# An adaLN block with linear attention and MoE: tail norms, routing and scatters between the last encoder steps, expert outputs scattered to token order

## The reference

```python
h = layernorm(x) * (1 + ca) + sa
x = x + ga * encoder(h)            # 4 layers
h = layernorm(x) * (1 + cb) + sb
x = x + gb * ffn(h)

# encoder layer: causal linear attention, 16 heads of 8, chunks of 128
q, k, v = h @ Wq + bq, h @ Wk + bk, h @ Wv + bv     # feature map elu + 1 on q and k
h = ln(h + attention(q, k, v) @ Wo + bo) * g1 + be1
h = ln(h + gelu(h @ W1 + b1) @ W2 + b2) * g2 + be2  # 512 hidden
# after the last layer: ln(h) * gf + bef

# ffn: 16 experts, two per token, 640 places per expert, plus a shared MLP
probs = softmax(h @ router_w + router_b)
vals, idx = top_k(probs, 2); vals = vals / (sum(vals) + 1e-9)
pos = (cumsum(one_hot(idx)) * one_hot(idx)).sum(1) - 1   # place in the expert, in token order
expert_in[idx, pos] += h * (pos < 640)
expert_out = (silu(expert_in @ wg) * (expert_in @ wu)) @ wd   # 176 hidden, per expert
out = h + shared_mlp(h) + sum over two of expert_out[idx, pos] * vals * (pos < 640)
```

## Time and profile before

| what | us |
| --- | --- |
| times of three runs | 1343.13, 1343.81 (median), 1349.38 |
| the profiled execution | 1346.05 |
| its span, first to last instruction | 1344.3 |
| PE busy in the span | 1049.5 (78%) |
| DVE busy | 970.3 (72%) |
| POOL busy | 895.0 (67%) |
| ACT busy | 580.2 (43%) |
| mean granted TensorE clock | 0.887 |

### The profile page before, as it was taken

One profiled execution on the slowest core, in us unless ns is written; L12 is line 12 of the kernel. 1 busy time (PEld: TensorE's weight loads), 2 busy tenths in 40 slices (PEclk: granted clock), 3 DMA queues, 4 the chain that ended last, 5 costly groups with the idle time before them and its releaser, 6 DMA issues.

```text
span 1344.3 us, 22639 instructions
## 1 busy us (share of the span) xinstructions
PE 1049.5 (78%) x4916; PEld 691.2 (51%) x4916; DVE 970.3 (72%) x2224; ACT 580.2 (43%) x1441; POOL 895.0 (67%) x1258
## 2 busy tenths in 40 slices
PE   2769899999998999899999999985326959999000
PEld 1445566656665666566656665654224536666000
DVE  3889789999999999999999999984654423332122
ACT  2335555555555555555555555544521112221000
POOL 4768877787778777887778777865827771000675
PEclk9889999999999999999999999998556969898555
DMA  8411010001000100010001000000002223331222
GB/s 237 164 63 72 24 39 23 23 31 39 23 23 31 39 23 23 31 39 23 28 26 39 23 31 23 31 16 17 16 4 73 81 66 111 110 106 55 66 70 60
DMA packets 53358, 68.20 MB, mean 51 GB/s; under 512 B 12184, under 2 KB 30024, under 8 KB 53200
## 3 DMA queue, kind: packets, MB, share of 16 engines
q1 hardware_dynamic: 44702, 54.21, 12.1%
q0 software_dynamic: 4096, 8.40, 2.2%
q10 hardware_dynamic: 4530, 5.26, 1.1%
HBM read 24.03 MB, written 16.80 MB: 30 GB/s over the span
## 4 chain that ended last, share of the span: by engine, by line
PE 37%; issue 19%; POOL 18%; DVE 16%; ACT 4%; DMA 3%; DVEq 1%; POOLq 1%; ACTq 0%; SPq 0%
PE ps L1141 10%; PE ps L1192 5%; POOL expert_in_scratch L693 4%; PE ps L1182 3%; POOL w L726 3%; DVE prod L1414 3%; PE ps L789 3%; PE ps L788 2%; DVE red L1427 2%; PE ps L1130 2%; POOL rstd L1068 2%; PE ps L739 2%; DVE kvm L1430 2%; PE ps L737 2%; POOL xg L1096 1%
## 5 line engine op out<-in xcount | busy, mean ns | idle before, releaser
L1141 PE MATMUL ps<-kv,tri 128*128 128x384 f32 x768 | 289.7, 516 | 2.3 <-DVE prod L1414 2.3
L1051 POOL TENSOR_TENSOR kv<-qk,v 128x1152 f32<-128x1152 f32 x128 | 280.4, 2191 | 2.9 <-DVE qk L1408 2.9
L1141 PEld LDWEIGHTS ps<-kv,tri 128*128 128x128 f32 x768 | 144.7, 202 | 101.1 <-issue 36.8
L1414 DVE TENSOR_TENSOR prod<-ps,qk 128x1152 f32<-128x1152 f32 x128 | 172.4, 1347 | 25.4 <-PE ps L1141 24.7
L1427 DVE TENSOR_REDUCE red<-prod 128x144 f32<-128x1152 f32 x128 | 172.0, 1344 | 3.3
L1192 PE MATMUL ps<-x1T,w1s 128*128 128x512 f32 x256 | 135.7, 612 | 8.0 <-ACT hT L1303 4.8
L1182 PE MATMUL ps<-w,hT 128*128 (+1 forms) x1024 | 137.9, 285 | 0.0
L1182 PEld LDWEIGHTS ps<-w,hT 128*128 128x128 f32 x1024 | 127.0, 195 | 1.5
L1437 DVE TENSOR_TENSOR att<-tot,rden 128x128 f32<-128x128 f32 x128 | 110.1, 860 | 7.0 <-DVE rden L1434 0.2
L1130 PE MATMUL ps<-wqkv,xT 128*128 (+1 forms) x256 | 111.3, 518 | 0.0
L1275 ACT ACTIVATE ex<-ps 128x256 f32<-128x256 f32 x128 | 48.6, 380 | 133.2 <-PE ps L1130 133.2
(11 more groups left out here) (215 smaller groups left out, 2295.4 us busy)
## 6 DMA issues: line engine op xcount, KB each, us to landing
x1s<-X SPq DMA_DIRECT2D x32, 256.0 KB, 2.3
w1s<-w SPq DMA_DIRECT2D x32, 256.0 KB, 2.3
xs<-X SPq DMA_DIRECT2D x31, 256.0 KB, 2.3
expert_in_scratch<-room SPq DMA_DIRECT2D x16, 320.0 KB, 3.4
kv<-expert_in_scratch SPq DMA_DIRECT2D x16, 320.0 KB, 2.9
expert_out_scratch<-kv ACTq DMA_DIRECT2D x16, 320.0 KB, 2.6
mod<-mod_scratch SPq DMA_DIRECT2D x1, 2304.0 KB, 8.9
x<-in_L_attn_x_dram SPq DMA_DIRECT2D x8, 256.0 KB, 5.9
```

Source lines behind the costliest of these rows:

```text
L1051: pool.tensor_tensor(kv[:, n, :].rearrange("p (e h d) -> p e h d", e=EV, h=H), qk[:, n, 1, :].rearrange("p (h d) -> p h d", h=H).unsqueeze ...
L1141: mm = pe.matmul(ps_cum[:, j, :], tri[:, :], kv[:, n, j * CB:(j + 1) * CB], start=True, stop=True)
L1414: dve.tensor_tensor(prod[:, :].rearrange("p (b e c) -> p b e c", b=3, e=3), ps_cum.rearrange("p b (e c) -> p b e c", e=3), qk[:, n, 0, :]. ...
```

## The change

Tail step j now stands behind body 28 + j (`FIRST_TAIL`), so tail steps 0 to 6 alternate with bodies 28 to 34, of which 28 to 31 are full bodies, and 7 to 10 follow. Routing goes in four groups of 8 tiles, behind tail steps 4, 6, 8 and 10; the counts of earlier groups are carried in `sel_before`. The scatter of row b stands behind tail step 5 + b (rows 6 and 7 behind the last), with its loads on SP and its indirect DMAs on POOL. The shared FFN and the experts still follow.

The scattered rows are 130 wide: h, the place in token order that the output has to go to (home), and the weight. `finish` multiplies by the weight that lies in `xes`; `home_rows` on DVE makes the list of destinations; POOL scatters each expert's output by 5 indirect DMAs to `expert_out_scratch`, now in token order and zeroed at the start by 16 DMAs of 256 KB. SP reloads a place of `xes` only when the transposes, the home rows and the finish of the expert that was in it are done. At the end each row takes two plain loads instead of 8 gathers, and three DVE operations of 512; ACT stores the result. `add_h` moves from POOL to DVE, inside experts 1 to 8. Second down-projections now use all 128 rows, padded with zeros, in place of 48. Some tiles get memory of their own (`hT_all`, `f_xn`, `g_xn`), and loops behind the encoder are unrolled.

```diff
+        FIRST_TAIL = STEPS - B + 4
+        GROUPS = ((0, 2), (2, 4), (4, 6), (6, 8))
...
-            with engine.Fori(4 * NT, (STEPS - 1) * NT, NT) as i:
+            with engine.Fori(4 * NT, FIRST_TAIL * NT, NT) as i:
                 body(i)
-            for k in range(STEPS - 1, STEPS + 3):
-                body(k * NT)
-                for j in DRAIN[k - STEPS + 1]:
-                    tail_step(j)
-            for j in range(DRAIN[-1][-1] + 1, B + 3):
-                tail_step(j)
-                if j == ROUTE_AFTER:
-                    route(0)
-            route(1)
+            for k in range(FIRST_TAIL, FIRST_TAIL + B + 3):
+                if k < STEPS + 3:
+                    body(k * NT)
+                j = k - FIRST_TAIL
+                tail_step(j)
+                for g in routed_after(j):
+                    route(g)
+                if j >= 5:
+                    scatter(j - 5)
+            for b in range(B - 2, B):
+                scatter(b)
...
+        def sp_rows(sp, b):
+            par = b % 2
+            if b == 0:
+                sp.wait_ge(p_done, TILES * L)
+            sp.wait_ge(q["h_ready"], b + 1)
+            wait(sp, scat[par], b // 2 * 128)
+            for k in range(2):
+                sp.dma_start(hs2[:, par, :, k, 0:D], Hr[:, b * NT:(b + 1) * NT, :]).then_inc(hs2_load[par], 16)
...
             def expert_rows(e, par):
                 wait(sp, q["xet_ps"], e - 1)
-                sp.dma_start(xes[:, par, :], xe_tiles[ds(e, 1)].rearrange("a p c -> (a p) c")).then_inc(xe_load[par], 16)
+                wait(sp, q["yidx_ready"], e - 1)
+                wait(sp, q["ye_sb"], e - 1)
+                sp.dma_start(xes[:, par, :, :].rearrange("p j c -> p (j c)"), xe_tiles[e]).then_inc(xe_load[par], 16)
...
             for par in range(2):
-                sp.wait_ge(scat[par], B * 64)
-            sp.wait_ge(q["ua_ps"], B)
+                sp.wait_ge(scat[par], B // 2 * 128)
+            sp.wait_ge(q["xsh_done"], TILES)
...
+            for b in range(B):
+                wait(sp, q["mix1_done"], b - 1)
+                for k in range(2):
+                    sp.dma_start(yg[:, b % 2, k, :, :], ye_tokens[b, :, k, :, :]).then_inc(yg_load[b % 2], 16)
...
+        def pool_scatter(pool, b):
+            par = b % 2
+            if b == 0:
+                pool.wait_ge(q["xe_zeroed"], 16 * E)
+            pool.wait_ge(q["route_ready"], b // 2 + 1)
+            wait(pool, scat[par], b // 2 * 128)
...
+            for n in range(NT):
+                for k in range(2):
+                    pool.indirect_dma_start(
+                        out=xe_dram, out_offset=bass.IndirectOffsetOnAxis(ap=scat_u[:, b * NT + n, k:k + 1], axis=0),
+                        in_=hs2[:, par, n, k, :], in_offset=None).then_inc(scat[par], 16)
...
+            for e in range(E):
+                par = e % 2
+                pool.wait_ge(q["yidx_ready"], e + 1)
+                pool.wait_ge(q["ye_sb"], e + 1)
+                for j in range(CT):
+                    pool.indirect_dma_start(
+                        out=ye_dram, out_offset=bass.IndirectOffsetOnAxis(ap=yidx[:, par, j:j + 1], axis=0),
+                        in_=yes[:, par, j, :], in_offset=None).then_inc(ysc[par], 16)
...
-                    mm = pe.matmul(o, ehid_b[0:FB, par, j * P:(j + 1) * P], ewd[0:FB, par, 1, :], start=False, stop=True)
+                    mm = pe.matmul(o, ehid_b[:, par, j * P:(j + 1) * P], ewd[:, par, 1, :], start=False, stop=True)
...
             def finish(e, par):
                 dve.wait_ge(q["ye_ps"], e + 1)
-                wait(dve, ye_store[par], ((e - par) // 2) * 16)
-                dve.tensor_copy(yes[:, par, 0:4 * P], down_bank[:, 0, :])
-                dve.tensor_copy(yes[:, par, 4 * P:CAP], down_bank[:, 1, 0:CAP - 4 * P]).then_inc(q["ye_sb"], 1)
+                wait(dve, ysc[par], e // 2 * CT * 16)
+                for j in range(CT):
+                    ins = dve.tensor_scalar(yes[:, par, j, :], down_bank[:, j // 4, (j % 4) * P:(j % 4 + 1) * P],
+                                            xes[:, par, j, D + 1:D + 2], None, ALU.mult)
+                ins.then_inc(q["ye_sb"], 1)
```

More of the change, by code:

```diff
@@ L252, in head_row, with steps @@
             return None
-        def steps(engine, body, head_step, tail_step, route):
+        def steps(engine, body, head_step, tail_step, route, scatter):
             head_step(0)
@@ L347, in adaln_block_kernel @@
         down_bank = ps[:, 6:8, :]
[L349 to L374, removed]
-        def sp_tail(sp):
[L378 to L386, removed]
+        def sp_rows(sp, b):
[6 more added lines that the diff above has]
+                sp.dma_start(hs2[:, par, :, k, 0:D], Hr[:, b * NT:(b + 1) * NT, :]).then_inc(hs2_load[par], 16)
+        def sp_tail(sp):
             def expert_weights(e, par):
-                wait(sp, q["ua_ps"], B + 2 * e - 2 if not isinstance(e, int) or e > 1 else 0)
-                gate, up = (w[ds(e, 1)].rearrange("a k f -> (a k) f") for w in (w_gate, w_up))
+                wait(sp, q["ua_ps"], B + 2 * e - 2 if e > 1 else 0)
+                gate, up = w_gate[e], w_up[e]
                 sp.dma_start(ewg[:, par, 0:F], gate).then_inc(ew_load[par], 16)
@@ new lines, in dve_route @@
+            dve.scalar_tensor_tensor(out=room_a, in0=before, scalar=float(CAP - 1), in1=over_tiles(expert_base),
+                                     op0=ALU.min, op1=ALU.add).then_inc(q["cnt_read"], 1)
+            dve.wait_ge(q["cnt_read"], g + 1)
+            if g < len(GROUPS) - 1:
+                then(dve.tensor_reduce(sel_row[:, :], selb[:, part, :].rearrange("p t e -> p e t"), AXX, ALU.add))
+                if g == 0:
+                    dve.tensor_copy(sel_before[:, :], sel_row[:, :])
+                else:
+                    dve.tensor_tensor(sel_before[:, :], sel_before[:, :], sel_row[:, :], ALU.add)
@@ L796, in expert @@
                 hidden(e, par, 0)
-                if not isinstance(e, int) or e > 0:
+                if e > 0:
                     down(e - 1, 1 - par)
-                if not isinstance(e, int) or e < E - 1:
+                if e < E - 1:
                     transposes(e + 1, 1 - par)
                 hidden(e, par, 1)
-            experts(pe, expert)
+            for e in range(E):
+                expert(e, e % 2)
             down(E - 1, 1)
@@ L812, in shared_gates @@
                 act.activation(sil_b[0:FB, :], ps[0:FB, 1, :], ACT.Silu).then_inc(q["esb_done"], 1)
-            rows(act, shared_gates, 1, B)
+            for r in range(B):
+                shared_gates(r)
             def turned(e, par):
@@ L920, in dve_tail, with mix_rows @@
-            rows(dve, mix_rows, 2, B)
+                    if half == 0:
+                        home_rows(e, par)
+                if 0 < e <= B:
+                    add_h(e - 1)
+            for e in range(E):
+                expert(e, e % 2)
+            finish(E - 1, 1)
+            def mix_rows(b):
+                par = b % 2
+                dve.wait_ge(yg_load[par], (b // 2 + 1) * 32)
+                wait(dve, q["mix2_done"], b)
+                dve.tensor_tensor(ymix[:, :, :], yg[:, par, 0, :, :], yg[:, par, 1, :, :], ALU.add).then_inc(q["mix1_done"], 1)
+                dve.wait_ge(q["mix1_done"], b + 1)
+                wait(dve, out_store[par], b // 2 * 16)
+                dve.tensor_tensor(yout[:, par, :, :], ymix[:, :, :], wide(mod[:, b:b + 1, 5, :]), ALU.mult).then_inc(q["mix2_done"], 1)
+                dve.wait_ge(q["mix2_done"], b + 1)
+                dve.tensor_tensor(yout[:, par, :, :], yout[:, par, :, :], X[:, tile_rows(b), :], ALU.add).then_inc(out_ready[par], 1)
@@ L922, in adaln_block_kernel @@
+            for b in range(B):
+                mix_rows(b)
         block = ctx.enter_context(nc.Block())
@@ L1117, in _ @@
             mm.then_inc(mod_ps, 1)
-            pe.wait_ge(consts_ready, 16)
+            pe.wait_ge(consts_ready, 19)
             def qkv(i, n):
```

378 lines of the change are left out of this document (170 added, 208 removed).

## The result

The changed kernel takes 1377.52 us (median of 4, 1376.31 to 1379.23) against 1344.12 us of the kernel before: a ratio of 1.0236, 95% interval 1.021 to 1.0262. It is slower, by 33.4 us where the prediction said 67. The profiled execution of the changed kernel has a span of 1376.4 us, 32.1 more than before.

What follows compares the result with a forecast made beforehand. PE and DVE were taken as both full in the encoder, PE as bounding the experts, POOL's gathers and DVE's mixing the end. 1344.3 + 58.6 + 67.6 - 58.8 = 1411.7, forecast as 1411 us, range 1339 to 1440.

Steps and rivals of the forecast that it cites:

- part 3: Expert stage: 14 reloads wait for finish, each 4.3 us of stall plus 1.6 of restart; 216.0 against 148.4, +67.6 us.
- The shared FFN: Behind all routing, on PE and DVE: 58.5 us, then 2.9 for the load of the first expert's rows.
- The expert: Expert stage: 8.2 us of base per expert at full clock, before stall and restart.
- The restart at the lower clock: After each PE stall, at joints and in experts: 1.6 us, from 9.8 less 8.2; 22.4 us over the experts.
- Rival 3: Expert stage: the clock doesn't pay, no restarts, 1389 us; counted within the forecast's 0.74.
- The joints: Tail steps behind bodies 28 to 31: in-order waits of 36.5 us, 42.9 with restarts; body 32 ends at about 953.
- From body 32 to the shared FFN: Tails, bodies 33 and 34, four routes and row 2's scatter in series: route 3 ends 139.4 us after body 32.
- part 5: The rest: zero writes and memsets at the start, add_h on DVE inside experts; taken as nothing.
- The end: After the last expert: scatters, landing and eight rows of plain loads take 42.0 us instead of 100.7, -58.8.
- Rival 1: Encoder tails hide, only bodies and last row count: experts from 1032, 1289 us; chance 0.11 with half-way cases.
- rival 2: Expert stage: the reload stays hidden, stage stays 148.4, time 1344 us; chance 0.08 with half-way cases.
- rival 4: Expert stage: the reload, contended by weights and scatters, lands in 5.9 us; 1453 us; chance 0.07.

Runs made afterwards that it cites:

- e2: The changed kernel with the second matmul of each down-projection back on 48 rows, the zeroing kept: 1415.72 us, ratio 1.0502 to the kernel before.
- e1: The kernel before with only the second matmul of each down-projection padded with zeros to 128 rows: 1305.95 us, ratio 0.9682.
- e4: The changed kernel with four extra matmuls, results unread, ahead of the waiting transposes in experts 1 to 14: 1346.46 us, ratio 0.998 to the kernel before.
- e5: The changed kernel with the tail steps four bodies later, none between two full bodies: 1358.03 us, ratio 1.0067 to the kernel before.
- e6: The changed kernel with weight and home columns copied out for an early reload, and four instead of two destination lists: 1280.68 us, ratio 0.9492 to the kernel before.
- e7: The changed kernel with early reload, four destination lists and tail steps four bodies later together: 1260.27 us, ratio 0.9341 to the kernel before.
- e8: The changed kernel with 48 rows in both matmuls of each down-projection, leaving out 80 hidden rows: 1383.02 us, ratio 1.025 to the kernel before.

## Why the prediction was right or wrong

**Direction, right.** Slower was forecast with 0.81, by the mechanism that the trace shows: PE waits in 14 experts for a load that is issued only behind finish.

**The size, wrong, by one step.** The step is the last sentence of part 3: "down with 128 instead of 48 rows streams the same columns: nothing". It was measured at 36 us in the changed kernel (e2 against it, 0.0266 of 1344) and 43 us in the kernel before (e1). The trace of before has the rows for it, 1122.02 to 1122.85 above, with the same 0.415 us between the starts as e2; I priced the edit from what it streams and did not look at the spacing. Two terms carry the error. The shared FFN: 58.5 and 2.9 of load were predicted from its first matmul to the first transposes, 46.1 were measured (1089.01 to 1135.07), 15.3 less; its 8 rows have 8 such matmuls each, and 64 x 0.19 = 12.2 of that is the spacing. With 48 rows again the same stretch takes 59.9 (e2, 1085.31 to 1145.16). The expert: 8.2 us of base were predicted, 6.30 is what e1 shows, and 10 x 0.19 = 1.9 is the spacing again.

**The restart at the lower clock, mis-sized the other way.** 1.6 us per stall were charged, from the two experts of the earlier trace rows; e4 gives 2.3. It hid part of the first error: 6.3 + 4.4 + 2.3 = 13.0 per expert, 13.2 measured, against a predicted 8.2 + 4.3 + 1.6 = 14.1. That the sum was nearer than its parts is luck. Rival 3, that the clock doesn't pay, is refuted.

**The joints, right in the path and in the sum.** 42.9 predicted, 6.4 of it restarts, 40.3 measured. One by one they are less even. A restart falls behind its joint, so it counts with the next one: 6.2, 9.9, 9.9 and 15.3 were predicted, 6.3, 7.5, 11.7 and 17.6 measured, and body 32, where the last restart was charged, gives 2.8 back. e5 confirms that they come from the place of the tails.

**From body 32 to the shared FFN, right.** The chain put the end of route 3 and with it the first shared matmul at 139.4 behind body 32; measured 1089.01 - 950.39 = 138.6. The steps between agree too: the second route (route 1) was expected to start 72.5 behind body 32 and starts at 74.9, the fourth (route 3) to end at 139.4 and ends at 136.6 (1086.97). Adding up many small waits, named as the largest risk, did no harm. One small term is missing: part 5 puts the three memsets at the start, but DVE zeroes the padding behind the fourth route, from 1087.03 to 1088.87, and the first shared matmul waits for that (5.4 us of waiting, most of it for the routing that stands ahead of the memsets in DVE's order). e2 keeps the memsets, so its 36 us do not contain them.

**The end, right within 4 us.** 42.0 predicted, 37.8 measured: 3.3 us per row were worked out from the highest rate in the page, which is no bound: the rows go by in 2.7 (1351.65 to 1373.6 for eight).

**The other rivals.** Rival 1 (tails hide) is refuted by the joints; rival 2 (reload hidden) and rival 4 (landing 5.9 us) by the 4.4 us of the waits. With the padding split off, the forecast of 1411 stands beside e2, 1415.7, or 1412 on the scale of the first comparison (1.0502 x 1344.12); but this too is luck in part: a front and an end that are 8.6 and 6.1 us shorter than predicted make up for an expert stage that is 13.0 longer (229.0 against 216.0, the clock at 0.73). The change is 33 us slower because it bundles a gain of some 36 with a loss of some 68.

## What to carry to other kernels

Price every edit of a bundle from the rows around it, also the one that looks like a side effect: here the spacing of two lines of matmuls held more than half of the predicted effect. When a buffer gets a second reader, look for what is queued behind its reload: ten columns copied out of it and two more list buffers turned a loss of 33 us into a gain of 68 (e6), and moving the tail steps to where no full engine waits behind them made it 88 (e7). Here a step that was moved between two full bodies cost its whole in-order chain through every engine that it uses, 6 to 18 us a joint.

## What the runs showed of the hardware that was not expected

A matmul that follows one with another number of rows starts 0.19 us later than it would otherwise, at full clock, with 128 columns of float32: 0.415 against 0.22 (the kernel before, e2, e8 and the changed kernel). Padding with zeros to the same number of rows removes that.

The clock rises when PE is given useless work: 0.78 to 0.98 over the expert stage in e4, and the kernel is 33 us faster for it. And in the kernel before it fell with hardly any idle time, 0.88 with PE busy for 144.81 of 151.2 us, while e1 with the padding has 0.97 at 103.45 of 107.14. What in the mixed row counts goes with the lower clock there stays open; no run tells it apart.
